# A vision block with routed experts on one core: drain reordered, experts chosen by groups, residual read back in pieces, attention products packed

## What is computed

```python
h = patches(x) @ W                                     # 2304 x 768 by 768 x 192
h = h + attention(layernorm(h), W_attn, b_attn, W_o, b_o)   # 64 images x 36 tokens, 12 heads of 16
flat = layernorm(h).reshape(-1, 192)
probs = softmax(flat @ router_w.T)
top_w, top_i = top_k(probs, 2); top_w = top_w / top_w.sum(-1, keepdims=True)
for e in range(8):
    w_e = sum(top_w * (top_i == e))
    out = out + w_e * (gelu(flat @ w1[e] + b1[e]) @ w2[e] + b2[e])
h = h + out
```

## Time and profile before

| | us |
|---|---|
| median of 3 runs | 444.54 (441.53 to 458.2) |
| the profiled execution | 444.34 |
| its span, first to last instruction | 442.4 |

### The profile page before, as it was taken

The page is one execution under the profiler, slowest core; times in us unless marked ns, Lnnn a source line. Parts: engine busy times, 40 slices in busy tenths (PEclk is TensorE's granted clock), DMA queues, the critical chain, the costliest instruction groups (busy, mean ns, idle before and its releaser), DMA issues.

```text
span 442.4 us, 14569 instructions
## 1 busy us (share of the span) xinstructions
PE 354.8 (80%) x5602; PEld 329.0 (74%) x5602; DVE 253.1 (57%) x638; ACT 219.8 (50%) x451; POOL 194.4 (44%) x236
## 2 busy tenths in 40 slices
PE   2788879998989899987622279799899898999920
PEld 2687779888989889877512169799899898999920
DVE  2566447787787766765349734455455455455417
ACT  3555648778888687753411024344344444344400
POOL 9005433446756664332630144465455455454220
PEclk9899999999999999975555579999999999999985
DMA  8757001444432333311006026621111111122039
GB/s 310 212 153 225 3 17 23 122 124 121 120 111 52 98 92 110 107 46 43 3 2 167 5 51 192 218 64 57 46 57 55 55 57 55 48 57 56 28 140 368
DMA packets 28654, 42.81 MB, mean 97 GB/s; under 512 B 12261, under 2 KB 18901, under 8 KB 28461
## 3 DMA queue, kind: packets, MB, share of 16 engines
q1 hardware_dynamic: 24460, 33.37, 25.0%
q0 software_dynamic: 4128, 8.50, 6.6%
HBM read 30.23 MB, written 9.67 MB: 90 GB/s over the span
## 4 chain that ended last, share of the span: by engine, by line
PE 45%; DVE 15%; issue 14%; POOL 10%; ACT 8%; DMA 6%; SPq 1%; POOLq 0%; DVEq 0%; ACTq 0%
PE PSA L1177 16%; PE PSA L1192 13%; PE PSA L958 4%; POOL XF L438 3%; POOL YP L450 2%; DMA REG<-xrows,KBR 2%; DMA W2l<-wqkv 2%; PE PSA L1015 2%; DVE H L947 2%; DVE REG L652 2%; PE PSA L1196 2%; PE PSA L1144 2%; DVE PTR L880 1%; PE PSA L990 1%; PE PSA L1041 1%
## 5 line engine op out<-in xcount | busy, mean ns | idle before, releaser
L1177 PE MATMUL PSA<-YT,W1h 128*128 128x128 f16 x774 | 79.4, 221 | 6.4 <-issue 4.7
L1177 PE MATMUL PSA<-YT,W1l 128*128 128x128 f16 (+1 forms) x516 | 76.6, 222 | 0.0
L482 POOL DMA_INDIRECT yrows<-KBR x43 | 43.9, 1022 | 69.0 <-DVE KBR L924 68.7
L1177 PEld LDWEIGHTS PSA<-YT,W1h 128*128 x774 | 64.6, 99 | 10.8 <-issue 5.5
L1192 PE MATMUL PSA<-W2h,PTR 128*128 x516 | 71.0, 246 | 0.3 <-DVE PTR L652 0.3
L638 ACT ACTIVATE PTR<-PSA 128x768 f32<-128x768 f32 x43 | 34.9, 811 | 69.3 <-PE PSA L1177 69.3
L1192 PE MATMUL PSA<-W2l,PTR 128*128 x258 | 63.5, 246 | 0.0
L477 POOL DMA_INDIRECT REG<-xrows,KBR x43 | 42.5, 987 | 43.0 <-DVE KBR L901 25.3
L643 ACT ACTIVATE PTR<-PTR 128x768 f16<-128x768 f32 x43 | 36.3, 843 | 46.2 <-PE PSA L1196 46.1
L652 DVE SCALAR_TENSOR_TENSOR PTR<-PTR 128x768 f16<-128x768 f32 x43 | 41.2, 958 | 25.9 <-ACT PTR L643 25.9
L958 PE MATMUL PSA<-W2h,REG 128*108 128x192 f16 x396 | 39.2, 261 | 17.7 <-DVE REG L652 17.6
(11 more groups left out here) (163 smaller groups left out, 794.6 us busy)
## 6 DMA issues: line engine op xcount, KB each, us to landing
WSTG<-w SPq DMA_DIRECT2D x16, 384.0 KB, 3.8
WSTG<-w SPq DMA_DIRECT2D x16, 336.0 KB, 3.2
REG<-xt SPq DMA_DIRECT2D x12, 324.0 KB, 4.5
W1l<-xt SPq DMA_DIRECT2D x10, 324.0 KB, 3.4
VB<-VP SPq DMA_DIRECT2D x99, 19.1 KB
hrows<-H SPq DMA_DIRECT2D x1, 1782.0 KB
H<-hrows SPq DMA_DIRECT2D x1, 1728.0 KB, 8.0
xrows<-REG SPq DMA_DIRECT2D x1, 1600.5 KB
```

The source lines that it names most:

```text
L482: gp.indirect_dma_start(out=yrows, out_offset=bass.IndirectOffsetOnAxis(ap=TARGET[:, s:s + 1], axis=0), in_=YO[s % 2], in_offset=None).the ...
L1177: ins = nc.tensor.matmul(bank(2 * u + f // (FC // 2), 128, FC // 2 * ST_)[:, w:w + ST_], weights[a, c], YT[0:rows, at:at + ST_], start=k = ...
```

## The change

Six things change.

- **Pieces earlier.** `AHEAD = 4` moves the conversion of the expert weights four steps ahead: the first six pieces fall into the embedding (ACT in steps -4 to -1: 1, 2, 1, 2 pieces), the last into step 17 (DVE 18).
- **Packing.** First norm, attention rows, WA and WO use the 128/64 split and `UP_PRODUCTS`: 5 matmuls for 6 in qk (four results), v and project; 3 transposes for 4. The bias sits in two rows of the low weights, converted as a seventh small tensor of one partition (`bqo`, 780 columns) and copied into place by four small transfers. POOL makes the low halves of the first norm and of the attention rows in two instructions each, and copies 64 rows of each transposed first norm (`norm1_again`); ACT evicts the transposed attention rows in two instructions.
- **Choice by groups.** The experts of tiles 0 to 3, 4 to 7 and 8 to 11 are chosen on DVE at the end of steps b+5 to b+9 (b the group's end); 12 to 15, 16 to 18 and 19 to 21 in the drain. A running sum (`PASSED_BY`) takes the place of the rank products: 3 matmuls for 44.
- **Drain.** The three drain steps are replaced by a list for each engine. Tiles 16 to 21 use PSUM banks that are free by then; the second norms of 18 to 21 have statistics of their own; DVE takes the attention rows' low half of tile 21 and the second norm's rows of tiles 20 and 21. In step 21 the probabilities are transposed before the router's products.
- **Counting.** The table parts are 16, 12, 10 and 6 columns for 11 each; which expert a tile belongs to (three DVE operations) is computed after the parts, and the first parts of the chain need one rank product.
- **Residual.** SP writes H for tiles 0 to 15 after step 21's scores, the rest with the last rows; it is read back in 6 transfers, each after another 3 expert tiles, the first after y_done 4.

```diff
         def pieces(i):
-            return range(max(0, 3 * i // 2), min(2 * PIECES, 3 * (i + 1) // 2))
+            return range(max(0, 3 * (i + AHEAD) // 2), max(0, min(2 * PIECES, 3 * (i + AHEAD + 1) // 2)))
...
-            sp.wait_ge(y_done, 1)
-            sp.dma_start(hrows.rearrange("(t p) c -> p t c", p=TT), H.rearrange("p (t c) -> p t c", c=C)).then_inc(h_stored, 16)
-            sp.wait_ge(h_stored, 16)
-            sp.dma_start(HS[:, 0:B * T // 128 * C], hrows[0:B * T, :].rearrange("(p j) c -> p (j c)", p=128)).then_inc(h_in, 16)
+            store_normed(OWN_BANKS, NT)
+            store_residual(OWN_BANKS, NT)
+            sp.wait_ge(h_stored, 16 * 2)
+            for at in range(0, B * T // 128, 3):
+                sp.wait_ge(y_done, 4 + at)
+                sp.dma_start(HS[:, at * C:(at + 3) * C], hrows[0:B * T, :].rearrange("(p j) c -> p (j c)", p=128)[:, at * C:(at + 3) * C]).then_inc(h_in, 16)
...
+            def norm1_again(t):
+                need(gp, n1_done, t + 1)
+                at = t % XRING * 4 * TT
+                nc.gpsimd.tensor_copy(XN[0:CB, at + HIGH_B_ONES * TT:at + (HIGH_B_ONES + 1) * TT],
+                                      XN[0:CB, at + BOTH_B * TT:at + (BOTH_B + 1) * TT]).then_inc(n1_again, 1)
...
-                nc.gpsimd.tensor_tensor(yp[:, C:2 * C], two(YF, t, C), yp[:, 0:C], ALU.subtract).then_inc(yl_done, 1)
+                y = two(YF, t, C)
+                nc.gpsimd.tensor_tensor(yp[:, C:LOW_A], y[:, CA:C], yp[:, CA:C], ALU.subtract).then_inc(yl_done, 1)
+                nc.gpsimd.tensor_tensor(yp[:, LOW_A:2 * C], y[:, 0:CA], yp[:, 0:CA], ALU.subtract).then_inc(yl_done, 1)
...
+            for i in range(-6, NT):
+                if has(i + 3):
+                    norm1_again(i + 3)
...
+                for g, (a, b) in enumerate(ROUTED):
+                    if b < OWN_BANKS:
+                        if i == b + 5:
+                            first_max(g)
+                        elif i == b + 6:
+                            first_place(g)
+                        elif i == b + 7:
+                            second_max(g)
+                        elif i == b + 8:
+                            second_place(g)
+                            passed_by(g)
+                        elif i == b + 9:
+                            gate_values(g)
...
+            def first_max(g):
+                a, b = ROUTED[g]
+                dve.wait_ge(lg_done, b)
+                nc.vector.tensor_reduce(best[:, a:b], by_expert(of_group(g, LG[:, :])), AX.X, ALU.max).then_inc(route, 1)
+                routed(g, 1)
+                nc.vector.tensor_tensor(by_expert(scratch(g, SAME[:, :])), by_expert(of_group(g, LG[:, :])), over_experts(best[:, a:b]), ALU.is_equal).then_inc(route, 1)
+                routed(g, 2)
+                nc.vector.tensor_tensor(by_expert(scratch(g, SAME[:, :])), by_expert(scratch(g, SAME[:, :])), expert_ids(g), ALU.mult).then_inc(route, 1)
...
+            def passed_by(g):
+                a, b = ROUTED[g]
+                for t in range(a, b):
+                    routed(g, CHOICES + t - a)
+                    nc.vector.tensor_tensor(PASSED_BY[:, (t + 1) * E:(t + 2) * E], PASSED_BY[:, t * E:(t + 1) * E],
+                                            CHOSEN[:, t * E:(t + 1) * E], ALU.add).then_inc(route, 1)
...
-                    n = 0
-                    for c in range(2):
-                        for a, b in PRODUCTS:
-                            ins = nc.tensor.matmul(bank(0, 128, 4 * TT)[:, j * TT:(j + 1) * TT],
-                                                   WA[a][:, c * WQKV + j * HC:c * WQKV + j * HC + 128], xn(t, b, c), start=n == 0, stop=n == 5)
-                            n += 1
+                    for k, (a, c, n) in enumerate(UP_PRODUCTS):
+                        x = xn(t, n)
+                        ins = nc.tensor.matmul(bank(0, 128, 4 * TT)[:, j * TT:(j + 1) * TT], WA[a][0:x.shape[0], c * WQKV + j * HC:c * WQKV + j * HC + 128], x,
+                                               start=k == 0, stop=k == len(UP_PRODUCTS) - 1)
...
-            for t in range(NT):
-                ins = nc.tensor.matmul(bank(7, ST_, E), ONES, CHOSEN[:, t * E:(t + 1) * E], start=t == 0, stop=t == NT - 1)
+            nc.tensor.matmul(bank(7, ST_, E), ONES, PASSED_BY[:, NT * E:(NT + 1) * E], start=True, stop=True).then_inc(rank_mm, 1)
```

522 lines of the change are left out of this document (348 added, 174 removed).

## The result

The changed kernel takes 448.2 us (median of 18 runs, 443.13 to 452.57) against 444.39 us for the kernel before in the same sessions. The ratio is 1.0078, with a 95% interval of 1.0041 to 1.0115: 0.8% slower, within 2%. I had said 446 in a range of 434 to 456. The profiled execution shown here is one of the longer ones, 450.25 us with a span of 448.4; the one of before had 442.4. Ratios and means over runs leave out executions more than 1.5% above their kernel's fastest; over all 18 of each the means are 447.0 before and 448.0 after.

A forecast was written before the change was run, and what follows sets the result against it. The prediction held PE's work and POOL's answering chain to be level in the steps, and the drain a chain of small operations. 444.3 + 0.5 + 1.8 + 2.4 - 1.9 + 0.3 - 1.1 = 446.3, said as 446; range 434 to 456.

The forecast's parts named there:

- The steps: Pipeline steps: +2.4 us in sum, bounds -9.2 and +8, as PE's saving lies mostly beside the chain through POOL.
- Four steps of each kind: nothing: Steps where POOL's round grows 0.5 us: the second norm's half ends later, PE's smaller work returns it; net zero.
- still about 6.3: Steps in which DVE converts a piece: length stays at about 6.3 us in the changed profile.
- step 14: Pipeline step with the choice's small DVE operations: priced at +0.9 us.
- Drain and choice: Step 20 to the slots: -1.9 us, slots at 234.5 for 236.38, bounds -6 and +1.5.
- stays near 213.4 (less 0.3): Drain: YF of tile 21 hardly moves, since tile 20's residual, sums and variances now stand ahead of it.
- 77 x 0.20 + 0.8 = 16.2: Drain: 77 mostly small dependent DVE instructions from tile 21's residual to counting take 16.2 us.
- Start and embedding: Before the first scores: +0.5 us for the further small tensor, +1.8 (0 to 3.3) for the earlier pieces on ACT.
- Tables and residual: Tables +0.3 us for three operations moved behind the last part; residual in pieces -1.1 (-1.5 to 0), removing a PE wait.
- PE sets the pace: Rival, steps: two thirds of PE's 9.2 us saving comes, drain gives -5; 434.5 us, 431 with all; chance 0.22.
- POOL becomes the bound: Rival, steps: second low-half instruction meets second piece (4.9 us), small choice operations block POOL (4.5); 455.7 us; chance 0.16.
- The drain does what its order suggests: Rival, drain: last logits 5 us earlier, small operations in waits, -5.5 for -1.9; 442.7 us; chance 0.20.

The follow-up runs named there:

- the first experiment: The changed kernel with PE's sixth product put back in qk, v and project (first product issued twice), against the changed kernel; ratio 1.0091 to before.
- the idle products: The changed kernel plus three unused PE products of 512 columns before the transposes of y in even steps 2 to 20; ratio 1.0017 to before.
- The short chain alone: The changed kernel, five products kept, with POOL's low half again one instruction and the fifth product's copy moved to ACT; ratio 1.0046 to before.
- the sixth product on top of it: The five-product kernel with POOL's one-instruction low half, with the first product of qk, v and project issued twice; ratio 0.9965 to before.

## Why the prediction was right, and where it was not

**The total** (446 for 448.2) was right, but in part by luck, as a sum of errors that cancelled: in the profiled execution the steps +10.5 us worse than forecast, the drain 5.0 better, the start 1.8 better.

**The steps, +2.4 forecast, +12.9 measured.** The failing step is the one in which I listed what PE's saving does: "there PE's smaller work behind it gives the same amount back. Four steps of each kind: nothing." That PE's saving would mostly lie beside the chain was right, and the first experiment confirms it as a sum. What I left out is that idle PE time is not free: I assumed a granted clock of 1.00 in the steps, though the earlier trace rows held a step at 0.58 with waits in it. The size of the omitted term can be read. The seven slowed steps took 55.8 us. The same steps at full clock in other profiled kernels that run the same lists there (steps 1 and 6 with the choice in fewer groups: 5.62, 7.30; steps 3, 5, 15 and 17 with the idle products: 6.29, 5.79, 6.20, 5.78; and 10 in the kernel with the pieces in their old steps: 7.94) sum to 44.9. The clock is 10.9 us, up to 1.2 less if step 6 would have been one of the longer ones (7.3 to 8.5 at full clock), and without it steps 0 to 19 would have taken 132.3, 2.0 more than before, for 2.4 forecast. This execution is 3.8 us longer than the mean of 446.4; if the clock makes that difference, its share in a mean execution is some 7 us, an estimate. The terms within that held in kind: 7.03 and 7.01 for 6.34 and 6.31 in steps 2 and 4 (I had named the mechanism, the second instruction meeting the second piece, only in a rival), 6.95 for 6.31 in step 8 as forecast (+0.7), step 14 +2.0 for +0.9, and single-piece steps 0 to 0.6 us shorter (6.30, 5.90, 6.20, 5.89 for 6.30, 6.47, 6.30, 6.16) where I had said "still about 6.3". POOL's low half took 0.73 alone, up to 1.23 beside one piece and up to 1.94 beside two, the copy 0.27 for 0.3.

The Trainium skill has the rule that I should have weighed: "TensorE: Matmul & The Clock Gate", section "A second HAM failure mode: psum-queue depth-cycling", says that short idle times between groups of products, not only long ones, can make the clock swing between its two levels. The trace agrees in kind: no wait of PE in these steps is longer than 1.8 us, and the clock fell all the same. Waits alone do not decide it: step 0 had the same 1.49 us in the changed kernel and with the choice in fewer groups, and step 1 behind it was at 0.57 in one and at 1.00 in the other.

**Drain and choice, -1.9 forecast, -6.9 measured.** Two terms were mis-sized. YF of tile 21 "stays near 213.4 (less 0.3)": measured from scores(20) it came 2.8 us earlier, since step 20 took 5.79 us at full clock for 8.59 at 0.58. I had credited the two pieces' 0.9 us but left the slow clock in. And "77 x 0.20 + 0.8 = 16.2" from the last residual to counting was 13.96: the list mixes operations of two groups, norms and logits, and independent neighbours start 0.07 to 0.12 us apart. The last residual's place (3.5 us after YF, 3.6 forecast), the slots (1.44, 1.30) and a DVE without idle time between them held.

**Start and embedding.** Forecast +2.3, +0.45 in this profile, about +3.2 as the mean over eight and six profiles. One execution is a poor measure of this stretch.

**Tables and residual.** +0.23 for +0.3; -0.71 for -1.1, and 2.0 in the one execution with it undone. There was no wait near the fourth expert tile.

**The rivals.** "PE sets the pace" failed by the first experiment: as a sum six products cost no more than five, and only steps such as 9 and 13 followed PE (6.18 for 5.90 and 5.89). "POOL becomes the bound" had the right sign for the steps and half the mechanism, at some 2 us and not 9.4 before the clock, and the small operations did block, but the other way: POOL holds DVE up (L921). "The drain does what its order suggests" (-5.5) was what the drain did.

What stays open: how much of packing's 8 us is the chain and how much the clock in the mean over executions. The short chain alone brought 0.3% of the 1.9% and the sixth product on top of it another 0.8%, all with intervals of 0.3 to 0.5% on either side.

## What to carry to other kernels

Count a wait on PE twice: once as time, and once as a risk for the granted clock of what follows. Here the second was worth more than the first (10.9 us and 2.0 in the profiled execution). In a stage where another engine's chain sets the pace, taking work off PE can slow the kernel, so shorten the chain first and take products away last. When small operations of one engine are interleaved with the steps of others, put them in the steps where that engine has slack, and not beside a string of GpSimd instructions.

## What the runs showed of the hardware

- The same instruction list ran a step in 5.62 us at a granted clock of 1.00 and in 7.96 at 0.57 in two executions. Profiles of one execution must be compared step by step at equal clock.
- Adding products made a kernel faster: 1.0046 to 0.9965 with PE's busy time in step 2 up from 5.51 to 5.87 us.
- A VectorE product of 108x32 elements took 1.50 us instead of 0.196 while GpSimd ran five instructions in a row, in four kernels at the same place; 0.50 us beside the first of three, in four others.
- VectorE's dependent small operations start 0.18 to 0.22 us apart, independent ones 0.07 to 0.12.
